# Attention and mixture of experts in one kernel: routing placed ahead of the first blocks' splits and norms, and the first gathers placed ahead of later experts' weights

## The reference

```
xn = layernorm(x)
# attention, per block
y = xn @ U; n = sum(y*y)                       # U: 128 x 32
attn = softmax(-(n_i + n_j - 2 y_i.y_j)); a = attn @ xn
# routing
logits = rmsnorm(xn) @ router_w.T              # 8 experts
top-2 of softmax(logits), weights scaled to sum 1
dispatch: the first 320 tokens of each expert, in order of tokens
# experts
gate = silu(xg @ rg); up = xg @ ru             # 128 -> 512, xg: gathered rows
routed += (gate * up) @ rd * weight            # 512 -> 128, added back by token
shared = (silu(xn @ sg) * (xn @ su)) @ sd      # 128 -> 1024 -> 128
out = x + a + shared + routed
```

## Time and profile before

| | us |
|---|---|
| median of 3 runs (lowest, highest) | 176.04 (175.55, 176.30) |
| the profiled execution | 176.18 |
| its span in the profile | 174.2 |
| TensorE matmuls busy (share) | 159.8 (92%) |
| VectorE busy | 123.4 (71%) |
| ScalarE busy | 103.9 (60%) |
| GpSimd busy | 78.7 (45%) |
| DMA queue issued by SyncE, share of 16 engines | 38.3% |
| mean granted TensorE clock | 0.98 |

### The profile page before, as it was taken

How to read it: one execution, slowest core, us unless ns; L and a number is a source line. 1 busy time by engine, 2 the same in 40 slices (tenths; PEclk the granted TensorE clock), 3 DMA queues, 4 the chain that set the end, 5 groups by cost and what they waited for, 6 DMA issues and landing times.

```text
span 174.2 us, 3188 instructions
## 1 busy us (share of the span) xinstructions
PE 159.8 (92%) x1003; PEld 139.8 (80%) x1003; DVE 123.4 (71%) x306; ACT 103.9 (60%) x220; POOL 78.7 (45%) x87
## 2 busy tenths in 40 slices
PE   6498999999999999999924999999999999989992
PEld 6486757796799988888813789999999999978892
DVE  4899869898763589999950367767678777644692
ACT  2358987962988278868620355779767665634200
POOL 5140430003777777877700000089898883456000
PEclk9999999999999999999996599999999999999999
DMA  5999959940111115634437100014322210117476
GB/s 159 317 205 148 254 157 278 348 137 0 61 52 61 42 49 162 191 93 149 132 100 217 44 4 0 2 48 122 120 64 80 74 39 18 32 38 200 119 249 195
DMA packets 26047, 20.73 MB, mean 119 GB/s; under 512 B 2253, under 2 KB 21736, under 8 KB 26032
## 3 DMA queue, kind: packets, MB, share of 16 engines
q1 hardware_dynamic: 24240, 17.89, 38.3%
q0 software_dynamic: 1792, 2.65, 4.8%
HBM read 12.36 MB, written 7.92 MB: 116 GB/s over the span
## 4 chain that ended last, share of the span: by engine, by line
PE 87%; DMA 5%; ACT 2%; DVE 2%; SPq 1%; issue 1%; DVEq 0%
PE bank L1080 15%; PE bank L1082 14%; PE bank L1081 14%; PE bank L1156 8%; PE bank L1198 8%; PE bank L1244 5%; PE bank L1246 5%; PE bank L1245 5%; DMA sw_raw<-in_L_ffn_su_dram 3%; PE bank L1129 2%; PE bank L1141 2%; PE bank L1260 2%; PE bank L1271 2%; DMA xg<-slots_dram 2%; PE bank L1095 1%; PE bank L1087 1%
## 5 line engine op out<-in xcount | busy, mean ns | idle before, releaser
L571 ACT ACTIVATE silu<-bank 128x512 f32<-128x512 f32 (+1 forms) x64 | 33.5, 523 | 41.1 <-PE bank L1082 41.0
L478 POOL DMA_INDIRECT slots_dram<-row,slot_i x32 | 35.1, 1096 | 27.6 <-issue 27.6
L899 DVE TENSOR_TENSOR bank<-bank,silu 128x320 f32<-128x320 f32 (+1 forms) x48 | 27.1, 565 | 25.0 <-ACT silu L571 13.8
L497 POOL DMA_INDIRECT routed_dram<-eo,xg x24 | 23.0, 959 | 12.3 <-DVE eo L939 6.4
L1080 PE MATMUL bank<-xnT_hi,sw_hi 128*128 128x512 f32 x64 | 26.9, 420 | 0.5 <-ACT silu L571 0.5
L905 DVE TENSOR_TENSOR hid_lo<-bank,hid_hi 128x320 fp32r<-128x320 f32 (+1 forms) x48 | 26.2, 547 | 0.0
L1082 PE MATMUL bank<-xnT_hi,sw_lo 128*128 128x512 f32 x64 | 25.8, 403 | 0.0
L1081 PE MATMUL bank<-xnT_lo,sw_hi 128*128 128x512 f32 x64 | 25.7, 401 | 0.0
L579 ACT CAST hid_hi<-bank 128x320 fp32r<-128x320 f32 (+1 forms) x48 | 23.1, 481 | 0.0
L485 POOL TENSOR_TENSOR ew_lo<-sw_raw,ew_hi 128x1024 fp32r<-128x1024 f32 x3 | 7.2, 2414 | 26.8 <-ACT ew_hi L595 26.8
L899 DVE TENSOR_TENSOR hid_s<-bank,silu 128x512 f32<-128x512 f32 x16 | 11.0, 689 | 8.1 <-PE bank L1082 7.2
(11 more groups left out here) (168 smaller groups left out, 322.0 us busy)
## 6 DMA issues: line engine op xcount, KB each, us to landing
sw_raw<-in_L_ffn_rg_dram SPq DMA_DIRECT2D x8, 256.0 KB, 2.6
sw_raw<-in_L_ffn_ru_dram SPq DMA_DIRECT2D x8, 256.0 KB, 3.0
rd_raw<-in_L_ffn_rd_dram SPq DMA_DIRECT2D x8, 256.0 KB, 3.1
routed_dram<-fill SPq DMA_DIRECT2D x1, 2048.0 KB, 11.6
routed<-routed_dram SPq DMA_DIRECT2D x8, 256.0 KB, 4.4
slots_dram<-fill SPq DMA_DIRECT2D x1, 1300.0 KB, 12.9
xg<-slots_dram SPq DMA_DIRECT2D x8, 130.0 KB, 2.3
acc<-in_L_attn_x_dram SPq DMA_DIRECT2D x4, 256.0 KB, 4.7
```

Of the source, the lines that this page charges most:

```text
L478: G.indirect_dma_start(slots_dram, bass.IndirectOffsetOnAxis(slot_i[:, k, t:t + 1], 0), row[:, t, 0:RW], None, bounds_check=E * CAP - 1, o ...
L497: G.indirect_dma_start(routed_dram, bass.IndirectOffsetOnAxis(xg[0:n, e % XB, r, 1:2].bitcast(I32), 0), eo[0:n, e % 2, r, :], None, bounds ...
L571: C.activation(silu[:, q % 2, 0:n], gate_b[q % 2][:, 0:n], ACT.Silu).then_inc(silu_ready, 1)
L899: V.tensor_tensor(hid, up[:, 0:n], silu[:, q % 2, 0:n], ALU.mult).then_inc(hid_ready, 1)
```

## The change

Four edits of order and one of layout. On VectorE the routing steps follow `lg_done` at once, with `mult_chunk` 4 to 7 between them, and `y_lo(0)`, `n_lo(0)`, `y_lo(1)`, `n_lo(1)` come behind `route_weights`. On TensorE `ranks` moves from between the output tiles to behind chunk 7, and three of the four output tiles of block 0 stand ahead of `project(2)` and `scores(0)`. On ScalarE `n_left(0)` goes behind the exponential for the weights, `n_hi(1)` and `y_hi(2)` go ahead of `exps(0)`, and within `y_hi` the squares come first. On SyncE the wait for `scattered` and the gathers of experts 0 and 1 come behind expert 4's down weights, ahead of the weights of expert 5; gathers 2 to 4 are ahead of expert 6's weights. `sel` is laid out as tokens by experts, so that VectorE writes it contiguously and the matmuls of `ranks` read it strided. Nothing that is computed changes.

```diff
--- before.py
+++ after.py
@@ -166,7 +166,7 @@
         z2 = sb("z2", [P, NT, E])
         key = sb("key", [P, NT, E])
         chosen = sb("chosen", [P, 2, NT, E])
-        sel = sb("sel", [P, E, NT], BF16)
+        sel = sb("sel", [P, NT, E], BF16)
         m1 = sb("m1", [P, NT])
         m2 = sb("m2", [P, NT])
         i1 = sb("i1", [P, NT])
@@ -390,14 +390,18 @@
                     sp.dma_start(routed[:, k, TG * g:TG * g + TG, :].rearrange("p t d -> p (t d)"), routed_v[k, g]
                                  ).then_inc(routed_loaded[k][g], 16)
 
-            for e in range(2, 6):
+            for e in range(2, 5):
                 next_expert_weights(e)
                 next_down(e)
-            next_expert_weights(6)
             sp.wait_ge(scattered, 16 * 2 * NT)
             sp.wait_ge(xg_padded, 1)
-            for e in range(XB):
+            load_slots(0)
+            load_slots(1)
+            next_expert_weights(5)
+            next_down(5)
+            for e in range(2, XB):
                 load_slots(e)
+            next_expert_weights(6)
             next_expert_weights(7)
             next_slots(5)
             next_down(6)
@@ -536,9 +540,9 @@
                 act.wait_ge(y_done, g + 1)
                 if g >= 2:
                     act.wait_ge(n_done, g - 1)
+                C.activation(ysq[:, g % 2, :], turn_b[g % 2][0:R, :], ACT.Square).then_inc(ysq_ready, 1)
                 C.copy(yL[0:3 * R, cols], turn_b[g % 2][0:3 * R, :])
                 C.copy(yR[0:3 * R, cols], turn_b[g % 2][0:3 * R, :]).then_inc(y_hi_s, 1)
-                C.activation(ysq[:, g % 2, :], turn_b[g % 2][0:R, :], ACT.Square).then_inc(ysq_ready, 1)
 
             def n_hi(g):
                 act.wait_ge(n_done, g + 1)
@@ -651,13 +655,13 @@
             silu_chunk(5)
             n_hi(0)
             silu_chunk(6)
-            n_left(0)
             silu_chunk(7)
             act.wait_ge(e2_asked, 1)
             C.activation(e2[:, :], m2[:, :], ACT.Exp).then_inc(e2_ready, 1)
-            exps(0)
+            n_left(0)
             n_hi(1)
             y_hi(2)
+            exps(0)
             n_left(1)
             n_hi(2)
             y_hi(3)
@@ -821,7 +825,7 @@
             def route_chosen():
                 settle()
                 then(V.tensor_tensor(chosen[:, 1, :, :], ids, per_token(i2[:, :]), ALU.is_equal))
-                V.tensor_tensor(sel[:, :, :].rearrange("p e t -> p t e"), chosen[:, 0, :, :], chosen[:, 1, :, :], ALU.add
+                V.tensor_tensor(sel[:, :, :], chosen[:, 0, :, :], chosen[:, 1, :, :], ALU.add
                                 ).then_inc(sel_ready, 1)
 
             def route_places():
@@ -992,24 +996,24 @@
             turned_lo(3)
             mult_chunk(2)
             mult_chunk(3)
-            y_lo(0)
             settle()
             route_logits()
             route_best()
+            route_first()
             mult_chunk(4)
-            route_first()
+            route_next()
+            route_second()
             mult_chunk(5)
-            n_lo(0)
+            route_chosen()
+            route_places()
             mult_chunk(6)
             mult_chunk(7)
-            route_next()
-            route_second()
-            route_chosen()
-            route_places()
+            route_slots()
+            route_weights()
+            y_lo(0)
+            n_lo(0)
             y_lo(1)
             n_lo(1)
-            route_slots()
-            route_weights()
             block_sum(0)
             dve.wait_ge(block_added, 1)
             y_lo(2)
@@ -1160,11 +1164,10 @@
 
             def ranks():
                 pe.wait_ge(sel_ready, 1)
-                s = sel[:, :, :].rearrange("p e t -> p (e t)")
-                M(bank[5][:, rank_cols], tri[:, :], s, start=True, stop=False)
-                M(bank[5][:, rank_cols], ones_f[0:1, :], slot0[0:1, :, :].rearrange("p e t -> p (e t)"),
-                  start=False, stop=True)
-                M(tot_ps, ones_bf[:, :], s, start=True, stop=True).then_inc(rank_done, 1)
+                s = sel[:, :, :].rearrange("p t e -> p e t")
+                M(rank_ps, tri[:, :], s, start=True, stop=False)
+                M(rank_ps, ones_f[0:1, :], slot0[0:1, :, :], start=False, stop=True)
+                M(tot_ps.rearrange("p (e t) -> p e t", e=E), ones_bf[:, :], s, start=True, stop=True).then_inc(rank_done, 1)
 
             def up_chunk(q, w_hi, w_lo, m_hi, m_lo):
                 n, up = width(q), up_bank(q)
@@ -1307,12 +1310,12 @@
             norms(0)
             for c in range(5, CS):
                 up_of_block(0, c)
+            ranks()
             norms(1)
+            down_first_block(range(0, TG - 1))
             project(2)
             scores(0)
-            down_first_block(range(0, 2))
-            ranks()
-            down_first_block(range(2, TG))
+            down_first_block(range(TG - 1, TG))
             norms(2)
             project(3)
             for b in range(B):
```

## The result

| | us |
|---|---|
| kernel before, median of 5 runs (lowest, highest) | 176.04 (175.55, 176.46) |
| changed kernel, median of 5 runs (lowest, highest) | 168.09 (167.95, 169.81) |
| ratio, 95% interval | 0.9583 (0.9542 to 0.9625) |
| predicted | 167.8 (166.9 to 171.0) |

The kernel is 7.9 us faster. The execution that was profiled is the one of 169.81 us. In the kernels of the experiments they differ again by a few lines.

The account below looks back on a forecast made before the run. TensorE is busy nearly throughout, so only its gaps can be won: 176.18 less the stall, 5.6, less the slow clock, 2.9, plus 0.1 for the front gives 167.8 us; range 166.9 to 171.0.

Parts of the forecast that it names:

- Stall, 5.6, and slow clock, 2.9: TensorE's wait for the first gathered rows, 5.6 us, and half clock behind it, 2.9 us; both go.
- Two things end nearly together, so both must move: SyncE's queue order and GpSimd's 32 scatters both hold the first gather, issued at 90.55; landing taken as 2.0 us.
- The scatters, moved: GpSimd's scatters start at 35.7 with earlier routing; the last ends at 79.5 and has landed at 81.5.
- The front, 0.1: Stages ahead of the gathers, with routing moved earlier: lateness there put at 0 to 1.0 us, taken as 0.1.
- `project(2)` with 0.1 to spare: VectorE releases `y_ready` 1 at 37.3 and TensorE reaches `project(2)` at 37.4, so no wait.
- ScalarE's order at nothing: `scores(1)` and norms need ScalarE's reordered copies; costed at nothing, as the tile held back and norms(2) cover it.
- Part 2: SyncE issues two gathers ahead of expert 5's weights: expert 0's rows at 84.8, TensorE at 88.3, 3.5 us to spare.
- The rule of exclusion: VectorE and GpSimd: by the page `n_lo(0)` could wait up to 0.97 us, sum 168.7; the rows say nothing, 167.8.
- B: Rival: late scatters or landing leave a stall up to 2.3 us, perhaps slow clock; 168.5 to 173 us, chance 0.10.
- C: Rival: VectorE late for `project(2)` or ScalarE for `scores(1)`, 0.5 to 1.0 each, perhaps 2.9 more; 168.7 to 171.5, chance 0.09.
- D: Rival: gathers are bound by scatters, which don't end earlier, so nothing moves; 176.2 us, chance 0.02.
- E: Rival: scatters under the attention stage are each held, 1.79 us a step, rows at 98.0; 180.3 us, chance 0.03.

Follow-up runs that it names:

- e0: The changed kernel run again unaltered; 168.82 us median of 6, ratio 0.9627 to the kernel before.
- e8: Kernel before with 75 unused matmuls of 128 columns, written out without a loop, ahead of the first turning of gathered rows; 175.5 us, ratio 0.9899.
- e1: Kernel before with SyncE's new queue order alone, routing and scatters as before; 169.37 us, ratio 0.9705.
- e9: Kernel before with all gathers moved ahead of expert 6's weights only, still behind expert 5's loads; 171.86 us, ratio 0.9743.
- e2: Changed kernel with SyncE's old queue order, so routing and scatters early but gathers behind expert 6's weights; 176.53 us, ratio 1.0061.
- e5: Changed kernel with all gathers behind expert 5's two loads and ahead of expert 6's; 169.09 us, ratio 0.9652.
- e7: Changed kernel with two output tiles instead of three ahead of `project(2)`; 169.9 us, ratio 0.9681.
- e6: Changed kernel with ScalarE's `exps(0)` back ahead of `n_hi(1)` and `y_hi(2)`; 168.99 us, ratio 0.9628.
- e11: e4 unchanged, run again on a chip where the kernel before takes 209.67 us; 201.37 us, ratio 0.9628.
- e4: Changed kernel with `sel` in its old layout, written strided by VectorE and read contiguously by TensorE; 167.61 us, ratio 0.955.
- e3: Kernel before with 80 unused matmuls of 128 columns, in a loop of five a turn, ahead of the first turning of gathered rows; 175.53 us, ratio 1.0014.

## Why the prediction was right, and where not

- *The total*: 167.8 predicted, 168.09 measured. Profiled executions with like starts: 176.18 - 168.03 = 8.15 us, against the 8.4 of the sum. Since both waits were moved at once, this total could not test the step that failed, below.
- *Stall, 5.6, and slow clock, 2.9*: right. TensorE reaches the turning at 88.63 in e0 and does not wait. From the turning to expert 0's first matmul the chain has 93.13 - 88.63 = 4.50 us, before it had 101.35 - 93.87 = 7.48: 2.98 less. Of these some 2.8 are the clock (e8). The other 0.2 belong to the wait itself: the three transposes behind a wait take 0.55 us at full clock too (e1, e8, e9), where they take 0.33 without one, and the working put all 0.57 of them down to the clock.
- *"Two things end nearly together, so both must move"*: wrong, and the one step of the mechanism that failed. The queue's order alone (e1) gives 6.6 of the 7.9 us, the routing alone (e2) loses 0.5, so that what the routing adds on top is 1.3. Two things that I held fixed move with the queue. The landing that I took as 2.0 is 1.15 when no weights are in flight, and the gather is 2.07 in place of 2.87: 1.65 us more than the 2.1 by which the issue would move with both held (2.0 behind the scatter's end is 88.45, against 90.55). Nor does the lower bound of 1.6 hold for e1: it was read from the last packets, and these come earlier there too. And the slow clock did not come with every stall: the clock stayed up at 1.2 (e5), 1.8 (e1) and 3.1 us (e9) and fell at 5.6 (before) and 5.9 (e2). So the queue alone collects 2.1 + 1.65 + 2.9 = 6.65. What remains is a stall of 1.8; less the 0.45 that the front pays for the routing, that is the routing's 1.3, nearly.
- *The scatters, moved*: right. In e0 the first starts at 35.85 (35.7 predicted), the last ends at 80.03 (79.5), lengthened by 3.8 us in all (some 3), against 31 steps of 1.27 and a scatter of 0.97, the first gather is at 82.06 (81.5). Landing 2.03 (2.0).
- *TensorE comes at 88.3, expert 0's first matmul at 92.9*: 88.63 and 92.97, the latter by TensorE's rows, where the kernel before has 101.19 (the chain, which counts from the end of the instruction ahead, has 93.13 and 101.35).
- *The front, 0.1*: mis-sized, 0.45. "Strided read taken as 0" was 0.3, from the end of the range kept for it. The tiles and `scores(1)` are slower than the rows they were costed by; over the whole stretch 0.15 of that stays.
- *`project(2)` with 0.1 to spare*: right. In the changed kernel's trace `n_lo(0)` ends 0.2 to 0.3 us ahead of it (in e0 at 37.49, and TensorE comes at 37.82), and e7 turns it into a wait of 1.5.
- *ScalarE's order at nothing, covered by the tile held back and `norms(2)`*: right, and the order does matter: e6 takes the cover away and pays 0.9.
- *Part 2, expert 5's weights later*: right. TensorE waits for none of them, and from expert 0's first matmul to the end it is 73.0 us in e0 and 72.5 in the other trace, 72.9 before.
- *The rule of exclusion* (Trainium skill, "SBUF — State Buffer", "Who interferes with whom": the second of two such instructions waits for the whole of the first). The sum by it would have been 168.7. Scatters that come second were held again (1.40 to 1.50 in place of 0.97), and a split of VectorE that comes second (L915 at 76.44, inside the scatter of 76.30) took 0.68 as ever. A VectorE tensor_scalar that comes second (L882) was longer once and once not: in e0 0.82 at 44.36, inside the scatter of 43.96, and 0.55 at 49.37, inside that of 49.07. Waiting out the whole scatter would have made it 1.1 and 1.2. So held in part at most; whether L882 runs in the two-port mode that the rule asks of a tensor_scalar no row shows.
- *Rivals.* B (a shorter stall stays) did not occur; e5, e9 and e1 make it on purpose and show it cheaper than I wrote, since the clock's 2.9 came with none of them. C (the front pays) did not occur as written, since nothing waits for VectorE or ScalarE there: the 0.45 come of the strided read and slower tiles. Its bounds don't follow from its terms either: 0.5 alone is 168.3, and 1.0 with 2.9 is 171.7, where it has 168.7 to 171.5. e7 shows that a gap of 1.5 there does not lower the clock. D and E were excluded by the scatters' times.

## To carry to other kernels

Read what stands ahead of a late transfer in its own queue before moving the work that produces its data: a load that waits for a buffer held up gathers it had nothing to do with, and moving it was most of the gain. A long stall of TensorE had a second price behind it here, and a cure of part of the stall collected that price whole, so the first of two bounds to go can be worth far more than the second. Where a mask is used as a moving operand, lay it out for TensorE if the engine that writes it has time.

## What the runs showed of the hardware that was not expected

- The granted clock was 1.00 behind idle stretches of 1.2, 1.8 and 3.1 us between long full stretches, and 0.50 behind 5.6 and 5.9 us.
- In the start, where TensorE is only partly busy between 6 and 10 us, the clock fell in some executions and not in others. From the first turning to `fold_logits` it took 14.5 to 14.6 us with the fall (15.9 in e11) and 13.0 to 13.3 without. The traces overlap in the length of the wait ahead of that turning (1.7 to 3.3 us with the fall, up to 2.6 without), so the wait alone does not decide; what does is open.
- The gather's issue followed the last scatter's end by 1.15 us with no other transfers in flight (e1), and by 2.00 to 2.21 with an expert's weights in flight (e0, e4, e6, e7, e9, the changed kernel). The gather took 2.07 us with nothing issued just ahead of it (e1), 2.36 in e9, 2.84 right behind expert 5's down weights (e5), and 2.86 to 3.20 behind expert 6's weights (before, e2, e8).
- A bf16 moving operand of 128 columns read at a stride of 16 bytes took 0.39 us instead of 0.23.
- A loop on TensorE cost 0.17 us of issue a turn (e3).
- On one chip three engines stood for some 34 us in the attention stage, and the profile names nothing of the kernel that they waited for.
